# Where the value product stands among the scores of a key tile

## The reference

```python
q = proj(query, Wq, bq)          # (B, H, S, Hd): 8, 16, 512, 16
k = proj(key, Wk, bk)
v = proj(value, Wv, bv)
q = q * cos + rotate_half(q) * sin
k = k * cos + rotate_half(k) * sin
attn = jnp.einsum('bhqd,bhkd->bhqk', q, k) * scale
attn_w = jax.nn.softmax(attn, axis=-1)
out = jnp.einsum('bhqk,bhkd->bhqd', attn_w, v)
out = jnp.einsum('bsd,ed->bse', out.transpose(0, 2, 1, 3).reshape(B, S, D), Wo) + bo
```

## Time and profile before

| | before |
|---|---|
| median of 3 runs | 642.36 us (642.34 to 644.07) |
| profiled execution, its own time | 644.45 us |
| its span, first to last instruction | 642.7 us |
| TensorE busy (matmul) | 570.9 us, 89% |
| VectorE busy | 558.4 us, 87% |
| ScalarE busy | 419.8 us, 65% |
| mean granted clock of TensorE | 0.955 |
| L835 maxima, VectorE | 512 of 676 ns |
| L805 exponentials, ScalarE | 512 of 598 ns |
| L695 value product, TensorE | 1024 of 594 ns |

### The profile page before, as it was taken

How to read it: one execution, slowest core, us unless ns; L and a number is a source line. 1 busy time by engine, 2 the same in 40 slices (tenths; PEclk the granted TensorE clock), 3 DMA queues, 4 the chain that set the end, 5 groups by cost and what they waited for, 6 DMA issues and landing times. The chain is left out here.

```text
span 642.7 us, 18901 instructions
## 1 busy us (share of the span) xinstructions
PE 570.9 (89%) x6478; PEld 271.5 (42%) x6478; DVE 558.4 (87%) x968; ACT 419.8 (65%) x774; POOL 269.8 (42%) x407
## 2 busy tenths in 40 slices
PE   4999997999899999999999999999999982888485
PEld 2655654234334444444434434434434421333164
DVE  2799999999999999999999999999899636598878
ACT  2667766157676676667667666667677680788694
POOL 4899896501333453223314215215205302599400
PEclk9999999579999999999999999999999998799888
DMA  8669876513322333422332233234222000000025
GB/s 290 199 169 283 238 220 166 150 47 74 79 51 67 77 61 58 76 65 50 64 82 52 52 82 65 50 65 77 56 54 47 3 1 2 1 1 0 1 87 177
DMA packets 61254, 55.19 MB, mean 86 GB/s; under 512 B 11040, under 2 KB 58784, under 8 KB 61216
## 3 DMA queue, kind: packets, MB, share of 16 engines
q1 hardware_dynamic: 61216, 54.70, 33.7%
HBM read 37.62 MB, written 16.78 MB: 85 GB/s over the span
## 5 line engine op out<-in xcount | busy, mean ns | idle before, releaser
L805 ACT ACTIVATE prob<-st_ps 128x512 f32<-128x512 f32 x512 | 276.1, 598 | 125.7 <-PE st_ps L673 124.9
L835 DVE TENSOR_REDUCE negm<-mx_ps 128x1 f32<-128x512 f32 x512 | 319.0, 676 | 25.8 <-PE mx_ps L682 23.6
L682 PE MATMUL mx_ps<-k,q 96*32 96x512 bf16 x2048 | 218.7, 399 | 8.3 <-DVE negm L835 4.7
L673 PE MATMUL st_ps<-q,k 98*32 98x512 bf16 x2048 | 211.7, 384 | 2.4 <-issue 1.1
L695 PE MATMUL pv_ps<-prob,v_u 128*32 128x512 f32 x1024 | 134.8, 594 | 8.8 <-DVE turned L844 5.2
L682 PEld LDWEIGHTS mx_ps<-k,q 96*32 96x32 bf16 x2048 | 62.3, 97 | 121.4 <-DVE negm L835 86.1
L673 PEld LDWEIGHTS st_ps<-q,k 98*32 98x32 bf16 x2048 | 66.7, 96 | 75.7 <-ACT prob L805 44.2
L1004 POOL TENSOR_TENSOR msplit<-negm,onesf 128x16 bf16<-128x16 f32 x32 | 7.1, 221 | 149.5 <-DVE negm L835 138.9
L1024 POOL TENSOR_TENSOR normal<-turned,recip 128x256 f32<-128x256 f32 x32 | 19.9, 621 | 102.1 <-DVE recip L850 102.1
L695 PEld LDWEIGHTS pv_ps<-prob,v_u 128*32 128x32 f32 x1024 | 32.4, 109 | 32.5 <-ACT prob L805 20.2
L299 POOL TENSOR_TENSOR parts<-work 128x512 bf16<-128x512 f32 x32 | 38.3, 1206 | 7.5 <-DVE work L287 6.0
(11 more groups left out here) (126 smaller groups left out, 694.0 us busy)
## 6 DMA issues: line engine op xcount, KB each, us to landing
qk_parts<-parts SPq DMA_DIRECT2D x96, 128.0 KB, 2.7
k<-qk_parts SPq DMA_DIRECT2D x192, 64.0 KB, 2.8
q<-qk_parts SPq DMA_DIRECT2D x192, 64.0 KB, 3.0
ctx<-in_ctxT SPq DMA_DIRECT2D x8, 512.0 KB, 4.4
X<-in_x SPq DMA_DIRECT2D x8, 512.0 KB, 8.4
out<-X SPq DMA_DIRECT2D x7, 512.0 KB, 2.9
q<-mrow SPq DMA_DIRECT2D x64, 4.0 KB, 2.6
wf<-in_w_down SPq DMA_DIRECT2D x1, 704.0 KB, 4.8
```

Source lines behind the costliest of these rows:

```text
L673: last = nc.tensor.matmul(st_ps[bank(i)][lo:lo + COLS, :], k6[g][:, h, kt * P + lo:kt * P + lo + COLS], q6[g][:, h, :], start=True, stop=True)
L682: last = nc.tensor.matmul(mx_ps[bank(i)][lo:lo + COLS, :], q6[g][0:ROWS, h, qt * P + lo:qt * P + lo + COLS], k6[g][0:ROWS, h, :], start=Tr ...
L805: nc.scalar.activation(prob[kt % 2][:, h, :], st_ps[bank(HPU * kt + h)][:], ACT.Exp, scale=SCALE).then_inc(exp_done, 1)
L835: nc.vector.tensor_reduce(negm[g % 2][:, h * TPB + qt:h * TPB + qt + 1], mx_ps[bank(TPB * h + qt)][:], op=ALU.max, axis=AX.X, negate=True) ...
```

## The change

In a key tile TensorE issued the value product of the key tile before behind the third head and ahead of the fourth. Now it issues all four heads first and the value product behind them. Nothing is added or removed, no other engine's program is touched, and all semaphores and the numbers that they are compared with stay.

```diff
--- before.py
+++ after.py
@@ -755,14 +755,13 @@
                         for kt in range(TPB):
 
                             for h in range(HPU):
-                                if h == HPU - 1:
-                                    if kt:
-                                        weigh(b, g, kt - 1)
-                                    elif not (is_first(b) and g == 0):
-                                        weigh(*((b, g - 1) if g else (b - 1, 3)), 3)
                                 scores(b, g, kt, h)
                                 if ahead:
                                     query_scores(mb, mg, kt, h)
+                            if kt:
+                                weigh(b, g, kt - 1)
+                            elif not (is_first(b) and g == 0):
+                                weigh(*((b, g - 1) if g else (b - 1, 3)), 3)
                             if is_last(b) and g >= 2 and 4 * (g - 2) + kt < NWT:
                                 weight_transpose(4 * (g - 2) + kt)
                             if is_last(b) and g == 3 and kt == 1:
```

## The result

The changed kernel took a median of 648.45 us (645.59 to 649.96, 8 runs) against 642.47 us (641.91 to 644.69, 8 runs) of the kernel before in the same comparison. The ratio is 1.0059, with a 95% interval of 1.0034 to 1.0083: slower by about 0.6%. The profiled execution took 649.64 us with a span of 647.8 us, against 644.45 and 642.7 us.

The account below looks back on a forecast made before the run. VectorE was taken to set the pace, lengthened when TensorE does something else for longer than three `mx_ps` banks last. Terms 3.5 + 0.3 + 2.0 = +5.8 us, put on the median of 642.36, gave 648.2 us; range 643.0 to 652.5.

Parts of the forecast that it names:

- Ordinary key tiles: Key tiles without a projection: the moved product just fits, 0 us; bounds nothing and 2 us.
- The projection: Thirteen VectorE gaps behind the output projection grow from 1.38 to about 1.65 us through a bank wait: +3.5 us.
- The turns of the batch loop: At seven turns, one VectorE wait of 0.62 us replaces two small gaps: +0.3 us; bounds -3.0 and +2.8.
- The last batch: Units 2 and 3: the fourth score waits for its bank without the product hiding it, +2.0 us; bounds 0 and 3.4.
- slack takes all of it up: First rival: VectorE recovers projection losses through denser tiles, about 643 us; chance 0.17 shared with a weak form of the forecast.
- The third rival: Tight key tiles give way too and the loop's cost may not hide: +10.3 us, 652.7 us; chance 0.13.
- The waits of the product for `turn_out`: Second rival: in key tile 1 these 5.2 us of TensorE waits go, shortening VectorE's gaps: -3.0 us, 639.4; chance 0.08.
- The bubble rule: Repeating gaps on the engine that should be saturated can mean too little PSUM; a fourth bank would matter more; no size.

Follow-up runs that it names:

- e3: Changed kernel with the value product back ahead of the fourth head at the 13 projections and in the last two units; 380.34 us stage, median 643.96 us, ratio 0.9982.
- e1: Changed kernel with the value product back ahead of the fourth head only in the 13 key tiles with a projection; 382.19 us stage, median 644.86 us, ratio 0.9999.
- e2: Changed kernel with the value product back ahead of the fourth score only in the last batch's units 2 and 3; 383.13 us stage, median 647.02 us, ratio 1.0014.
- e10: Changed kernel, product between fourth score and fourth query scores at 13 projections, ahead of fourth score in last two units, projection in quarters; stage 375.70 us, ratio 0.9905.
- e12: Fastest version (product moved at projections and in last two units, projection in quarters) timed again without edit; 375.78 us stage, median 638.43 us, ratio 0.9929.
- e4: Changed kernel with the projection cut into four quarters spread over key tiles 1 and 2, residual moved to key tile 3; 379.68 us stage, ratio 0.9979.
- e5: The changed kernel run again without any edit; 385.07 us stage against 385.02, median 647.97 us, ratio 1.0063 to the kernel before.
- e6: Changed kernel, product between fourth score and fourth query scores in all key tiles with query scores, ahead of fourth score in last two units; stage 381.51 us, ratio 1.0008.
- e11: Fastest version with the last three quarters further apart (heads 0 and 2 of key tile 2, head 0 of 3), residual in mid key tile 3; stage 379.81 us, ratio 0.9982.
- e8: Changed kernel, product between fourth score and fourth query scores everywhere, ahead of fourth score in last two units, projection in quarters; stage 383.11 us, ratio 1.0048.

## Why the prediction was right

The direction, the mechanism and the range hold. That the median of 648.45 us lies within 0.3 us of the forecast of 648.2 is luck: the stage lengthened by 4.40 us, not by 5.8, and the ratios of 1.0059 and 1.0063 mean about 4 us, where the forecast's 5.8 us would be a ratio of 1.0091, above the upper end of both intervals (1.0083 and 1.0088). The forecast stood on a median of the kernel before of 642.36 us, which came out between 642.76 and 644.71 in the comparisons of the experiments. Point by point:

- **Ordinary key tiles: zero.** Wrong in sign, and outside the stated bounds, which went from nothing upwards. In a batch the visible gaps grew from 3.24 us (2 x 1.38 + 0.20 + 0.28) to 3.87 (1.64 + 1.63 + 0.60), and yet the batch grew only from 50.18 to 50.42 us: of 0.63 us, 0.39 came back. One stop fewer is worth 0.09 of it, the other 0.3 us or so are waits too short to be marked: the six maxima behind a projection take 3.77 us before and 3.67 after, the ten of unit 0 6.35 and 6.22. In the trace of the kernel before, five of these six start 0.60 us apart and the last (305.02) 0.69 us behind its neighbour; between 182 and 500 us there are 26 such pairs 0.69 to 0.72 us apart, in the changed kernel none. VectorE's timeline of the kernel before:

```profile
286.33 6.35 DVE L835 TENSOR_REDUCE negm<-mx_ps 128x1 f32<-128x512 f32 x10
...
301.94 3.77 DVE L835 TENSOR_REDUCE negm<-mx_ps 128x1 f32<-128x512 f32 x6
```

and of the changed kernel:

```profile
288.25 6.22 DVE L834 TENSOR_REDUCE negm<-mx_ps 128x1 f32<-128x512 f32 x10
...
304.10 3.67 DVE L834 TENSOR_REDUCE negm<-mx_ps 128x1 f32<-128x512 f32 x6
```

e3 shows the same from the other side, as a stretch 0.64 us shorter than before.

- **The projection, +3.5 us.** The mechanism came out step for step, in us behind `turn_out`: 1.34, 1.57, 2.43 and 4.37, forecast 1.33, 1.55, 2.41 and 4.36; gap 1.64, forecast 1.65. e1 confirms it by undoing it, with 2.83 us for the thirteen. The size was taken too large by what the denser tiles give back: from one `turn_out` to the next the loss is not 0.27 but 0.21 us in unit 1 (13.08 to 13.29) and 0.15 in unit 2 (13.70 to 13.85).
- **The turns of the batch loop, +0.3 us.** The shape is right: one gap of 0.60 (forecast 0.62), the second gone, and the loop's own cost hidden beside the product: in the trace the first score of the new unit starts at 283.24, 0.86 us behind the product (282.38), as inside a unit. The sign of the sum is not: the unit at the turn went from 12.18 to 12.09 us in batches 2 to 5, and the seven turns together come to about -0.1 us. In batch 0 the changed kernel has two gaps of 0.28 us at ends of units 0 and 1 (the maxima at 147.09 and 159.03 us) that the forecast had counted as filled: neither `turn_back` nor the statistics run there in batch 0.
- **The last batch, +2.0 us.** Right. With the thirteenth projection, 2.27 us were forecast and 2.42 measured; e2 gives 1.84 of them back. Key tile 2 of unit 2 went from 2.40 to 2.84 us (forecast 2.82). Key tile 3 went from 2.47 to 3.33 us, its fourth score starting at 1.59 (forecast +0.86 and 1.59).
- **Rivals.** That slack takes all of it up is refuted by e1, where undoing one place moves the whole stage. But it holds in part: 0.39 of the 0.63 us a batch. The argument against it, that VectorE is never idle in between, overlooked the short waits that the rows do not mark. The third rival, that the tight key tiles give way too and the loop's cost stays, did not come: between 182 and 508 us all 20 gaps of VectorE lie behind a projection or at a turn. The waits of the product for `turn_out` were indeed gone up to the last batch, and it was worth nothing, since a wait for the maxima's bank had taken their place. Only the version that removes both and cuts the projection gains clear of the noise (e10 and e12).

The bubble rule of the Trainium skill (Perfetto Trace Analysis, Optimization Strategy) speaks of too little PSUM. e10 shows that the same banks do with smaller pieces: the repeated 1.64 us fell to one gap of 0.13 and three of 0.18 us. A fourth bank for the maxima was not tried, so what it would give is not shown; the kernel holds eight banks in this stage and uses all of them (three `mx_ps`, three `st_ps`, `pv_ps`, `misc_ps`).

The 1.00 us ahead of the first `turn_out` goes at least in part with the granted clock of the first 60 us, and not with the change. In the traces the clock was 0.94 there in the changed kernel and in e4, and TensorE's first maxima tile started at 112.0 and 112.6 us; 0.97 in ten others, e5 among them, with 110.4 to 111.7 us; and 1.00 in e6 and e11, with 108.9 and 109.6 us. Why the clock differed is open.

## What to carry to other kernels

Where a consumer lives from a small stock of buffers, ask of each piece on the producer how long it is with its direct neighbours, and which buffer the instruction ahead of it must wait for. Here moving a piece past an instruction that waits for a buffer swapped one wait for another. Cutting the longest piece gained more here (e10, 4.9 us of the stage under the kernel before) than any order of whole pieces (e3, 0.3 us), but only where the cuts left no long stretch around the other pieces (not in e8 and e11).

## What was not expected of the hardware

A stop of VectorE costs about 0.09 us more than its length: neighbouring maxima of 0.68 us start 0.60 us apart, and one that stands alone occupies 0.69 us. This is worked out from the rows; no run isolates it. The stage's length repeated to 0.05 us between two executions (385.02 and 385.07 us) and to 0.08 us between two on different chips (375.70 and 375.78 us), while whole times of one kernel in one comparison ranged over more than 4 us.
